# Scores of four head groups in one go in a shifted-attention stage, and its bias product moved to the second group

## The chip, the cores and the metric

The kernel runs on one core of one Trainium2 chip. The metric is the device time of one launch in microseconds (us). Three runs of the kernel before gave 1269.83, 1270.92 and 1271.11 us; their median is 1270.92 us.

## The reference, cut to what matters

The whole program is an audio tower: a convolutional tokenizer with its own attention, a shifted-window attention, a slice attention, a bidirectional GRU and a mixture of experts, each added to the running activations `h` of shape (64, 128, 64). The change touches the shifted-window attention alone. Its input is the layernorm of `h` (64 sequences of 128 rows by 64 channels); with a sequence as long as the window there is no shift and no mask:

```python
qkv = x @ qkv_weight.T + qkv_bias            # 64 sequences, 8 heads of 8 channels
attn = einsum("whqd,whkd->whqk", q * 8 ** -0.5, k) + bias_table[rel_idx]   # 128 x 128 for each head
attn = softmax(attn, axis=-1)
out = einsum("whqk,whkd->wqhd", attn, v) @ proj_weight.T + proj_bias
```

All is in float32.

## The kernel before

The program is written by hand, one instruction list for each engine, with semaphores between them. In the attention stage (stage 2) the 64 sequences are taken two at a time: 32 pairs of sequences, and since a loop turn `i` holds two of them (lanes `l` = 0 and 1), 16 turns. The two sequences of a pair have 16 heads in all, 4 in each of four head groups `u` = 0 to 3. A group's scores are 128 queries by 4 x 128 keys, one PSUM bank. A turn has eight slots `t` = 4 l + u, one for each group. `pipelined` writes turn 0 out, loops over turns 1 to 14, and writes turn 15 and a draining turn out.

What each engine does for group t, and in which slot:

- GpSimd, slot u = 2, for the next pair: `spread` (L614) multiplies the keys `a_k` with a mask, so that `a_kz` holds in each quarter of 32 partitions the keys of four heads, 512 columns. It waits for the keys and for all scores of the pair before (`a_sc_r`).
- TensorE: `scores` (L690) multiplies one quarter of 32 rows of `a_q` with the same quarter of `a_kz`: 32 x 128 by 32 x 512, into the bank `scores_bank(t)`. Before the change groups t+1 and t+2 are multiplied in each odd slot; groups 0 and 1 of a pair come in the last slot of the pair before, groups 2 and 3 in slot u = 1.
- The position bias is added by VectorE for groups 0, 1 and 2: `tensor_tensor_reduce` (L852), four instructions of 128 x 128, adds it, stores the sum in `a_P` and takes the extreme of each row. For group 3 TensorE adds it: `bias` (L696) multiplies the identity with the 512 columns of the bias table into the same bank, in slot u = 2, and VectorE takes the extremes in one instruction (`tensor_reduce`, L848) from the bank.
- ScalarE, one slot later: four exponentials with row sums (L799), from `a_P`, or for group 3 from the bank.
- VectorE, two slots later: reciprocal of the sums (L837); GpSimd: `normed` (L620) multiplies the probabilities.
- TensorE, three slots later: four transposes (L739) into bank 4; VectorE (even groups, L861) or ScalarE (odd groups, L804) copies them out.
- TensorE, four slots later: `attended` (L709), probabilities by values; after group 3 VectorE copies them (L868).
- For the next pair: `rows` (L668, transpose of the rows, slot 0; copied by ScalarE at L776), `qkv` (L674 to L676, slot 1), queries by ScalarE (L780) and keys by VectorE (L830, slot 1), values by ScalarE (L786, slot 3). For the pair before last: `project` (L721, slot 0), added to `h` by VectorE (L874).
- Once in a turn VectorE centres rows for the next layernorm (L275, L277, slot 5, behind the keys) and takes their variance (slot 7), ScalarE squares them (L284, slot 6), and GpSimd makes the inverse roots (L293, L295).

Each engine works through its slots strictly in the order written. In a slot TensorE has: transposes of the group three back, values (`attended`) of the group four back, qkv (slot 1), scores (odd slots), bias (slot 2); in slot 0 rows and the projection come behind the transposes, ahead of `attended`.

In stage 1a the convolutions (L159 and L171) use the array in the same way as the scores: products of 32 rows by 512 columns in four row quarters, into four banks.

Of the kernel before, what the change touches and what calls it, by code (L numbers as in the profile page):

```python
# [59 lines left out]
def build(nc, xp, consts, out):  # L60
# [8 lines left out]
    def c(name, a=0, b=None):  # L69

        o, w = ON[name]
        return cst[:, o + a:o + (w if b is None else b)]

    eye = c("eye")
# [501 lines left out]
    def exists(i, d, last=N2 - 1):  # L576

        return not isinstance(i, int) or 0 <= i + d <= last
# [16 lines left out]
    def scores_bank(t):  # L595
        return bank(SBANK[t % 4])
# [65 lines left out]
    def stage2_pe(pe, start=None):  # L662
        def rows(i, l):
            pe.wait_ge(a_xs_r, i * 2 + (l + 1))

            if l or exists(i, -1):
                pe.wait_ge(a_v_r, i * 2 + l)
            nc.tensor.transpose(bank(2)[:, 0:128], xs[l], eye).then_inc(a_t_r, 1)  # L668

        def qkv(i, l):  # L670
            pe.wait_ge(a_xT_r, i * 2 + (l + 1))

            pe.wait_ge(a_h_r, i * 2 + (l + 1))
            nc.tensor.matmul(bank(2)[:, 128:256], c("a_q"), xT[l], start=True, stop=True)  # L674
            nc.tensor.matmul(bank(3)[:, 0:128], c("a_k"), xT[l], start=True, stop=True)
            nc.tensor.matmul(bank(2)[:, 256:384], xT[l], c("a_v"), start=True, stop=True).then_inc(a_qkv_r, 1)  # L676

        def scores(i, t):
            l, u = t // 4, t % 4
            if u == 0:  # L680
                pe.wait_ge(a_q_r, i * 2 + (l + 1))
                pe.wait_ge(a_kz_r, i * 2 + (l + 1))
            if t >= 4 or exists(i, -1):

                if u == 3:
                    pe.wait_ge(a_e_r, i * 8 + (t - 3))
                else:
                    pe.wait_ge(a_mx_r, i * 8 + (t - 3))
            r = slice(32 * u, 32 * u + 32)
            m = nc.tensor.matmul(scores_bank(t), a_q[l][r, :], a_kz[l][r, :], start=True, stop=u != 3)  # L690
            if u != 3:
                m.then_inc(a_sc_r, 1)

        def bias(t):

            nc.tensor.matmul(scores_bank(t), eye, c("a_bias", 512, 1024), start=False, stop=True).then_inc(a_sc_r, 1)  # L696

        def attended(i, t):
            l, u = t // 4, t % 4
            if u % 2:  # L700
                pe.wait_ge(a_pta_r, i * 4 + (t // 2 + 1))
            else:
                pe.wait_ge(a_ptd_r, i * 4 + (t // 2 + 1))
            if u == 0:
                pe.wait_ge(a_v_r, i * 2 + (l + 1))

                pe.wait_ge(a_oT_r, i * 2 + (l + 2))
            for j in range(4):
                m = nc.tensor.matmul(bank(6)[32 * j:32 * j + 32, 128 * u:128 * u + 128], a_v[l][:, 128 * u + 32 * j:128 * u + 32 * j + 32],  # L709
                                     a_PT[t % 4][:, 128 * j:128 * j + 128], start=True, stop=True)  # L710
            m.then_inc(a_av_r, 1)

        def project(i, l):

            pe.wait_ge(a_oT_r, i * 2 + (l + 1))

            pe.wait_ge(a_h_r, i * 2 + (l + 1))
            for s in range(2):
                for g in range(2):
                    for half in (0, 64):  # L720
                        m = nc.tensor.matmul(bank(3)[half:half + 64, 128 + 64 * s:192 + 64 * s],  # L721
                                             a_oT[l][:, 128 * (2 * s + g) + half:128 * (2 * s + g) + half + 64], a_pp[:, 64 * g:64 * g + 64],
                                             start=(g == 0), stop=(g == 1))
            m.then_inc(a_pr_r, 1)

        def slot(i, t):
            l, u = t // 4, t % 4
            if i_is(i, 0) and t == 1:

                pe.wait_ge(b_h, ND)  # L730
            ib, tb = back(i, t, 3)
            if exists(ib, 0):
                pe.wait_ge(a_n_r, ib * 8 + (tb + 1))
                if tb % 2:
                    pe.wait_ge(a_ptd_r, ib * 4 + (tb // 2 + 1))
                elif tb or exists(ib, -1):
                    pe.wait_ge(a_pta_r, ib * 4 + tb // 2)
                for k in range(4):
                    m = nc.tensor.transpose(bank(4)[:, 128 * k:128 * (k + 1)], a_P[tb % 4][:, 128 * k:128 * (k + 1)], eye)  # L739
                m.then_inc(a_pt_r, 1)  # L740
            ib, tb = back(i, t, 4)
            if u and exists(ib, 0):
                attended(ib, tb)
            if u == 1 and exists(i, l, N2 - 1):
                qkv(i + l, 1 - l)
            if t % 2:
                for d in (1, 2):
                    if exists(i, (t + d) // 8):
                        scores(i + (t + d) // 8, (t + d) % 8)
            if u == 2 and exists(i, 0):  # L750
                bias(t + 1)
            if u == 0:
                if exists(i, l, N2 - 1):
                    rows(i + l, 1 - l)
                if exists(i, -1, N2 - 1):
                    project(i, l)
                if exists(ib, 0):
                    attended(ib, tb)
            if isinstance(i, int) and i == N2 and t < 2:
                stage3_pe(pe, start=t)  # L760
        if start == 0:
            rows(0, 0)
            return
        if start == 1:
            qkv(0, 0)
            return
        pe.wait_ge(f_dve, SETUP3)
        pe.wait_ge(m_loaded, LOADED7)
        scores(0, 0)
        scores(0, 1)  # L770
        pipelined(pe, slot)

    def stage2_act(act, start=None):
# [15 lines left out]
        def slot(i, t):  # L789
            l, u = t // 4, t % 4  # L790
            ib, tb = back(i, t, 1)
            if exists(ib, 0):
                act.wait_ge(a_mx_r, ib * 8 + (tb + 1))
                if tb % 4 == 3 and (tb >= 4 or exists(ib, -1)):
                    act.wait_ge(a_pt_r, ib * 8 + (tb - 3))
                for k in range(4):
                    P = a_P[tb % 4][:, 128 * k:128 * (k + 1)]
                    raw = scores_bank(tb)[:, 128 * k:128 * (k + 1)] if tb % 4 == 3 else P
                    m = nc.scalar.activation(P, raw, ACT.Exp, bias=a_mx[tb % 4][:, k:k + 1], scale=-1.0, accum_out=a_sm[tb % 4][:, k:k + 1])  # L799
                m.then_inc(a_e_r, 1)  # L800
            ib, tb = back(i, t, 3)
            if tb % 2 and exists(ib, 0):
                act.wait_ge(a_pt_r, ib * 8 + (tb + 1))
                nc.scalar.copy(a_PT[tb % 4], bank(4)).then_inc(a_pta_r, 1)  # L804
            if u == 0 and exists(i, l, N2 - 1):
                rows(i + l, 1 - l)
            if u == 1 and exists(i, l, N2 - 1):
                queries(i + l, 1 - l)
            if u == 3 and exists(i, l, N2 - 1):
                values(i + l, 1 - l)  # L810
            if i_is(i, 0) and t in (2, 4):
                g = LATE[t // 2 - 1]
                square(act, g + 1, 8 * g, 8, g % 2)
            if t == 6 and exists(i, -1):
                square(act, i + LN[1], i * 4 - 4, 4, 0)
            if isinstance(i, int) and i == N2 and t in (0, 2):
                stage3_act(act, start=t // 2)
# [9 lines left out]
    def stage2_dve(v, start=None):  # L827
# [4 lines left out]
        def slot(i, t):  # L832
            l, u = t // 4, t % 4
# [6 lines left out]
                v.wait_ge(b_c3, ND)  # L840
            if exists(i, 0):

                v.wait_ge(a_sc_r, i * 8 + (t + 1))
                if u != 3 and (t >= 4 or exists(i, -1)):
                    v.wait_ge(a_pt_r, i * 8 + (t - 3))

                if u == 3:
                    m = nc.vector.tensor_reduce(a_mx[t % 4], scores_bank(t).rearrange("p (j k) -> p j k", j=4), X, ALU.min)  # L848
                else:
                    nc.vector.memset(spare[:, 24 + t:25 + t], 0.0)  # L850
                for k in range(0 if u == 3 else 4):
                    m = nc.vector.tensor_tensor_reduce(a_P[t % 4][:, 128 * k:128 * (k + 1)], scores_bank(t)[:, 128 * k:128 * (k + 1)],  # L852
                                                       c("a_bias", 512 * (u % 2) + 128 * k, 512 * (u % 2) + 128 * (k + 1)), 1.0, 3e38,
                                                       ALU.add, ALU.min, a_mx[t % 4][:, k:k + 1])
                m.then_inc(a_mx_r, 1)
# [1476 lines left out]
```

## Time and profile before

| | us |
|---|---|
| median of the three runs | 1270.92 |
| the profiled execution, its own time | 1270.48 |
| its span on the core | 1268.2 |
| TensorE busy (matmuls) | 1169.8, 92% of the span |
| VectorE busy | 846.8, 67% |
| ScalarE busy | 757.4, 60% |
| GpSimd busy | 618.4, 49% |

The span is the time from the first to the last instruction that the profile holds; the rest of the execution's time lies around it. An engine's busy time sums what its records cover; records of TensorE overlap, so that a busy TensorE is not one at its peak. The granted clock is the share of TensorE's full clock that it was given in a stretch: 1.00 is 2.4 GHz, 0.50 is 1.2 GHz. In lists, PE is TensorE, DVE VectorE, ACT ScalarE, POOL GpSimd, and L690 is line 690 of the kernel. The value behind an arrow in square brackets is the idle time of the engine just before the group, and what ended it.

### The profile page before, as it was taken

To read this page: it belongs to the slowest core of one execution; us is meant where nothing else is said; L and a number is where in the kernel's file an instruction comes from. 1 tells how busy PE (TensorE), PEld (TensorE's weight loads), DVE (VectorE), ACT (ScalarE), POOL (GpSimd) and SP (SyncE) were. 2 spreads that over 40 slices of the span, in tenths; PEclk is the share of its full clock that TensorE was granted. 3 is DMA by queue.
4 is the path that set the end of the run, shared out by engine and by line. 5 is a ranking of instruction groups with operands and counts; after the bars stand their busy time and mean duration, and the time that the engine had idled before them with its cause. 6 is when DMAs were issued, how large, how long until landed. Compare 5 with 4: busy or idle time off the path is not lost.

```text
span 1268.2 us, 43497 instructions
## 1 busy us (share of the span) xinstructions
PE 1169.8 (92%) x16184; PEld 806.1 (64%) x16184; DVE 846.8 (67%) x2765; ACT 757.4 (60%) x2435; POOL 618.4 (49%) x939
## 2 busy tenths in 40 slices
PE   7989989999999979999999998899999999789997
PEld 3447745555555547787878877677777764456665
DVE  5965667777777767787787876555555555746664
ACT  0137678888888855555555554566666666544553
POOL 6012567676667753555565565233333332245455
PEclk9988989999999989999999999999999999889999
DMA  6000000000000000000000000000000000000000
GB/s 229 1 1 2 2 2 1 0 0 0 0 0 0 0 2 3 2 0 0 0 0 0 0 0 2 2 1 0 0 0 0 0 1 1 1 5 16 17 17 18
DMA packets 10833, 10.26 MB, mean 8 GB/s; under 512 B 9232, under 2 KB 9872, under 8 KB 10640
## 3 DMA queue, kind: packets, MB, share of 16 engines
q1 hardware_dynamic: 10768, 9.35, 2.5%
q8 instruction: 46, 0.75, 0.3%
q14 instruction: 19, 0.16, 0.0%
HBM read 7.25 MB, written 2.10 MB: 7 GB/s over the span
## 4 chain that ended last, share of the span: by engine, by line
PE 65%; issue 12%; POOL 11%; DVE 6%; ACT 4%; POOLq 1%; DMA 0%; SPq 0%; ACTq 0%; DVEq 0%
PE bank L1489 8%; POOL big L620 7%; PE bank L1837 5%; PE bank L1171 5%; PE bank L1855 5%; PE bank L1484 5%; PE bank L1160 3%; PE bank L1472 3%; PE bank L159 3%; PE bank L1249 3%; PE bank L1180 3%; PE bank L1198 2%; PE bank L1602 2%; PE bank L1239 2%; PE bank L1219 2%
## 5 line engine op out<-in xcount | busy, mean ns | idle before, releaser
L620 POOL TENSOR_TENSOR big<-big 128x512 f32<-128x512 f32 x128 | 132.9, 1039 | 55.7 <-DVE big L837 55.7
L799 ACT ACTIVATE big<-big 128x128 f32<-128x128 f32 x384 | 148.9, 394 | 0.5 <-DVE big L852 0.5
L1074 POOL TENSOR_TENSOR big<-big 128x512 f32<-128x512 f32 x64 | 65.6, 1045 | 127.3 <-DVE big L1348 127.3
L1570 POOL TENSOR_TENSOR big<-g_a,g_b 64x64 f32 x128 | 40.1, 313 | 172.4 <-DVE g_a L1560 172.4
L1551 DVE TENSOR_TENSOR_SCAN g_t<-g_zero_r,bank 128x128 f32<-128x128 f32 x128 | 53.8, 420 | 87.6 <-ACT g_zero_r L1536 87.6
L739 PEld LDWEIGHTS bank<-cst,big 128*128 128x128 f32 x512 | 57.2, 142 | 76.6 <-issue 59.9
L1758 POOL TENSOR_TENSOR big<-big 128x512 f32<-128x512 f32 x48 | 61.0, 1270 | 72.9 <-DVE big L1961 70.3
L1891 ACT ACTIVATE big<-bank 128x512 f32<-128x512 f32 x128 | 66.1, 604 | 48.7 <-PE bank L1837 48.7
L1536 ACT ACTIVATE g_zero_r<-bank,g_bias 128x64 f32<-128x64 f32 x128 | 40.7, 318 | 90.0 <-PE bank L1489 89.9
L852 DVE CUSTOM_DVE_ANT_0 big<-bank,cst 128x128 f32<-128x128 f32 x384 | 88.4, 286 | 6.9 <-issue 6.9
L690 PE MATMUL bank<-big 32*128 32x512 f32 x256 | 76.1, 646 | 15.2 <-POOL big L614 8.0
L739 PE MATMUL bank<-cst,big 128*128 128x128 f32 x512 | 83.7, 286 | 3.6 <-POOL big L620 2.9
L1489 PEld LDWEIGHTS bank<-g_b,cst 128*64 128x64 f32 x1024 | 40.3, 136 | 57.9 <-DVE g_b L1558 57.6
L1171 PEld LDWEIGHTS bank<-big 128*128 128x128 f32 x512 | 61.2, 196 | 24.3 <-issue 23.5
L1855 PEld LDWEIGHTS bank<-cst,big 128*64 128x64 f32 x2048 | 62.4, 138 | 18.5 <-issue 17.4
L799 ACT ACTIVATION_READ_ACCUMULATOR big<-big 128x1 f32 x384 | 74.0, 193 | 0.0
L1489 PE MATMUL bank<-g_b,cst 128*64 128x64 f32 x1024 | 57.9, 234 | 10.9 <-DVE g_b L1558 10.6
L1855 PE MATMUL bank<-cst,big 128*64 128x64 f32 x2048 | 66.6, 223 | 0.0
L1294 ACT ACTIVATE big<-big 128x1024 f32<-128x1024 f32 x32 | 33.9, 1059 | 54.7 <-DVE big L1339 54.7
L1171 PE MATMUL bank<-big 128*128 128x96 f32 x512 | 66.5, 284 | 0.0
L1837 PE MATMUL bank<-big,cst 64*128 64x512 f32 x256 | 65.9, 631 | 0.0
L1961 DVE TENSOR_TENSOR big<-bank,fB 128x512 f32<-128x512 f32 x64 | 44.3, 692 | 30.1 <-PE bank L1855 28.5
(274 smaller groups left out, 3216.5 us busy)
## 6 DMA issues: line engine op xcount, KB each, us to landing
cst<-consts_dram SPq DMA_DIRECT2D x1, 3364.5 KB, 14.2
out_dram<-h SPq DMA_DIRECT2D x8, 256.0 KB, 2.6
big<-x_dram SPq DMA_DIRECT2D x3, 512.0 KB, 5.8
cst<-consts_dram SPq DMA_DIRECT2D x3, 256.0 KB
big<-x_dram SPq DMA_DIRECT2D x1, 513.0 KB, 4.2
big<-consts_dram SPq DMA_DIRECT2D x4, 96.0 KB, 2.2
cst<-consts_dram SPq DMA_DIRECT2D x4, 48.0 KB, 2.0
g_ih_exchanged<-consts_dram SPq DMA_DIRECT2D x2, 96.0 KB, 7.3
```

What stands on the lines that cost most here:

```text
L620: nc.gpsimd.tensor_tensor(P, P, a_rs[t % 4].unsqueeze(2).to_broadcast([128, 4, 128]), ALU.mult).then_inc(a_n_r, 1)
L690: m = nc.tensor.matmul(scores_bank(t), a_q[l][r, :], a_kz[l][r, :], start=True, stop=u != 3)
L739: m = nc.tensor.transpose(bank(4)[:, 128 * k:128 * (k + 1)], a_P[tb % 4][:, 128 * k:128 * (k + 1)], eye)
L799: m = nc.scalar.activation(P, raw, ACT.Exp, bias=a_mx[tb % 4][:, k:k + 1], scale=-1.0, accum_out=a_sm[tb % 4][:, k:k + 1])
L852: m = nc.vector.tensor_tensor_reduce(a_P[t % 4][:, 128 * k:128 * (k + 1)], scores_bank(t)[:, 128 * k:128 * (k + 1)], c("a_bias", 512 * (u ...
L1074: nc.gpsimd.tensor_tensor(w, w, f_rs[l][:, 8 * s:8 * s + 8].unsqueeze(2).to_broadcast([128, 8, 64]), ALU.mult).then_inc(f_w_r, 1)
L1171: m = nc.tensor.matmul(regions()[:, k // 4, k % 4, :], f_w[l][:, 128 * k:128 * k + 128], f_xs1[l][:, 96 * (k // 4):96 * (k // 4) + 96], st ...
L1484: nc.tensor.matmul(to[:, ::-1, 1, :] if s else to[:, :, 0, :], w, x, start=((half == 0 or gate == 2) and s == 0), stop=True, skip_group_ch ...
L1489: m = nc.tensor.matmul(to[64 * d:64 * d + 64, :], c("g_hh", 128 * gate + 64 * d, 128 * gate + 64 * d + 64), state[:, :], start=start, stop ...
L1837: nc.tensor.matmul(hidden_bank(s, e), c("m_w1", 128 * e, 128 * e + 128)[64 * s:64 * s + 64], m_xT[l][64 * s:64 * s + 64, :], start=True, s ...
L1855: m = nc.tensor.matmul(out_bank(e)[64 * half:64 * half + 64, 64 * (2 * p + s):64 * (2 * p + s) + 64], hidden(e, s)[:, 128 * p + 64 * half: ...
L1891: nc.scalar.activation(hidden(e, s), hidden_bank(s, e), ACT.Relu).then_inc(m_ra, 1)
```

## The change

The scores of a pair's four groups are multiplied one behind the other in slot 0 of the pair itself, ahead of everything else of TensorE in that slot, each in its own row quarter and into its own bank. The one bias product goes from group 3 to group 1 and stands right behind them. VectorE's single reduction and ScalarE's exponentials from the bank go to group 1 with it; group 3 is now treated as groups 0 and 2 are. The waits of the scores are changed: they wait for the maxima of all four groups of the pair before and the exponentials of its group 1. VectorE's group 0 waits for the first of the four products, the other groups for all of them and the bias. The wait for the end of stage 1b (`b_h`) moves from slot 1 to slot 0.

```diff
-        def scores(i, t):
-            l, u = t // 4, t % 4
-            if u == 0:
-                pe.wait_ge(a_q_r, i * 2 + (l + 1))
-                pe.wait_ge(a_kz_r, i * 2 + (l + 1))
-            if t >= 4 or exists(i, -1):
-
-                if u == 3:
-                    pe.wait_ge(a_e_r, i * 8 + (t - 3))
-                else:
-                    pe.wait_ge(a_mx_r, i * 8 + (t - 3))
-            r = slice(32 * u, 32 * u + 32)
-            m = nc.tensor.matmul(scores_bank(t), a_q[l][r, :], a_kz[l][r, :], start=True, stop=u != 3)
-            if u != 3:
-                m.then_inc(a_sc_r, 1)
-
-        def bias(t):
-
-            nc.tensor.matmul(scores_bank(t), eye, c("a_bias", 512, 1024), start=False, stop=True).then_inc(a_sc_r, 1)
+        def scores(i, l):
+
+            pe.wait_ge(a_q_r, i * 2 + (l + 1))
+            pe.wait_ge(a_kz_r, i * 2 + (l + 1))
+            if l or exists(i, -1):
+                pe.wait_ge(a_mx_r, i * 8 + 4 * l)
+                pe.wait_ge(a_e_r, i * 8 + (4 * l - 2))
+            for u in range(4):
+                r = slice(32 * u, 32 * u + 32)
+                m = nc.tensor.matmul(scores_bank(u), a_q[l][r, :], a_kz[l][r, :], start=True, stop=u != 1)
+                if u != 1:
+                    m.then_inc(a_sc_r, 1)
+
+            nc.tensor.matmul(scores_bank(1), eye, c("a_bias", 512, 1024), start=False, stop=True).then_inc(a_sc_r, 1)
...
-            if i_is(i, 0) and t == 1:
+            if i_is(i, 0) and t == 0:
 
                 pe.wait_ge(b_h, ND)
+            if u == 0 and exists(i, 0):
+                scores(i, l)
...
-            if t % 2:
-                for d in (1, 2):
-                    if exists(i, (t + d) // 8):
-                        scores(i + (t + d) // 8, (t + d) % 8)
-            if u == 2 and exists(i, 0):
-                bias(t + 1)
...
-        scores(0, 0)
-        scores(0, 1)
         pipelined(pe, slot)
...
-                if tb % 4 == 3 and (tb >= 4 or exists(ib, -1)):
+                if tb % 4 == 1 and (tb >= 4 or exists(ib, -1)):
                     act.wait_ge(a_pt_r, ib * 8 + (tb - 3))
                 for k in range(4):
                     P = a_P[tb % 4][:, 128 * k:128 * (k + 1)]
-                    raw = scores_bank(tb)[:, 128 * k:128 * (k + 1)] if tb % 4 == 3 else P
+                    raw = scores_bank(tb)[:, 128 * k:128 * (k + 1)] if tb % 4 == 1 else P
...
-                v.wait_ge(a_sc_r, i * 8 + (t + 1))
-                if u != 3 and (t >= 4 or exists(i, -1)):
+                v.wait_ge(a_sc_r, i * 8 + (4 * l + (4 if u else 1)))
+                if u != 1 and (t >= 4 or exists(i, -1)):
                     v.wait_ge(a_pt_r, i * 8 + (t - 3))
 
-                if u == 3:
+                if u == 1:
                     m = nc.vector.tensor_reduce(a_mx[t % 4], scores_bank(t).rearrange("p (j k) -> p j k", j=4), X, ALU.min)
                 else:
                     nc.vector.memset(spare[:, 24 + t:25 + t], 0.0)
-                for k in range(0 if u == 3 else 4):
+                for k in range(0 if u == 1 else 4):
```

## Rows read from the trace of the kernel before

**Rows 1.** Busy time by stretch; columns: PE, PEld, DVE, ACT, POOL, granted clock, DMA

```profile
160.00:200.00 40.00, 34.90 (x248) 18.09 (x244) 26.65 (x149) 30.20 (x140) 24.70 (x28) 0.87 0.01 2
200.00:440.00 240.00, 226.52 (x2114) 126.51 (x2114) 177.82 (x1009) 209.97 (x986) 170.02 (x213) 1.00 0.00 0
```

**Rows 2.** Waits, 200 to 440 us: total us, times, longest

```profile
POOL big L620 <- DVE big L837: 42.7, 39, 1.9
...
POOL big L614 <- PE bank L696: 25.8, 27, 1.3
...
ACT big L780 <- PE bank L676: 17.8, 26, 0.7
```

**Rows 3.** Timeline of TensorE's matmuls, one pair; columns: start us, length us

```profile
301.07 1.23 PE L690 MATMUL bank<-big 32*128 32x512 f32 x4 [0.43 <-issue]
302.23 0.66 PE L739 MATMUL bank<-cst,big 128*128 128x128 f32 x4
...
304.97 0.49 PE L674 MATMUL bank<-big,cst 128*128 128x128 f32 x2
...
305.83 1.13 PE L690 MATMUL bank<-big 32*128 32x512 f32 x4
306.89 0.66 PE L739 MATMUL bank<-cst,big 128*128 128x128 f32 x4
...
307.84 1.12 PE L696 MATMUL bank<-cst 128*128 128x512 f32 x2
308.81 0.60 PE L739 MATMUL bank<-cst,big 128*128 128x128 f32 x4
...
310.33 0.81 PE L690 MATMUL bank<-big 32*128 32x512 f32 x2 [0.57 <-POOL big L614]
```

**Rows 4.** Timeline of the other engines in the same pair

```profile
305.94 0.37 ACT L780 ACTIVATE big<-bank,a_bqs 128x128 f32<-128x128 f32 x1 [0.72 <-PE bank L676]
...
306.20 0.39 ACT L799 ACTIVATE big<-big 128x128 f32<-128x128 f32 x1
...
307.08 0.17 DVE L837 RECIPROCAL big<-big 128x4 f32<-128x4 f32 x1
...
307.34 1.04 POOL L620 TENSOR_TENSOR big<-big 128x512 f32<-128x512 f32 x1 [1.93 <-DVE big L837]
...
307.74 0.56 ACT L804 COPY big<-bank 128x512 f32<-128x512 f32 x1
...
309.05 1.04 POOL L614 TENSOR_TENSOR big<-big,a_mask 128x512 f32<-128x512 f32 x1 [0.67 <-PE bank L696]
```

**Rows 5.** Groups by shape, 200 to 440 us: count, busy us, mean ns

```profile
L739 PE MATMUL bank<-cst,big 128*128 128x128 f32 x420 | 67.7, 283 | 0.0
...
L799 ACT ACTIVATE big<-bank,big 128x128 f32<-128x128 f32 x108 | 38.2, 369 | 0.3
```

**Rows 6.** Timeline of TensorE in stage 1a, four products in four row quarters

```profile
60.12 1.14 PE L159 MATMUL bank<-big,cst 32*128 32x512 f32 x8 [0.96 <-DVE big L207]
```

**Rows 7.** Busy time by stretch in the stage's filling, clock in the third column from the end

```profile
170.00:173.20 3.20, 3.20 (x20) 2.27 (x20) 1.73 (x12) 1.82 (x10) 2.84 (x3) 0.50 0.00 0
...
183.60:190.30 6.70, 6.70 (x25) 3.12 (x24) 1.84 (x13) 4.03 (x18) 1.27 (x2) 0.50 0.01 2
```

**Rows 8.** Timeline of TensorE in the stage's filling

```profile
165.55 0.66 PE L739 MATMUL bank<-cst,big 128*128 128x128 f32 x4 [1.08 <-POOL big L620]
...
182.10 0.66 PE L739 MATMUL bank<-cst,big 128*128 128x128 f32 x4 [1.51 <-POOL big L620]
...
184.20 2.08 PE L690 MATMUL bank<-big 32*128 32x512 f32 x4
186.21 1.12 PE L739 MATMUL bank<-cst,big 128*128 128x128 f32 x4
...
187.84 2.08 PE L696 MATMUL bank<-cst 128*128 128x512 f32 x2
189.71 0.92 PE L739 MATMUL bank<-cst,big 128*128 128x128 f32 x4
```

## The prediction

> **What bounds the kernel now.** I read the stage's stretches first. Shifted attention runs from about 160 to 455 us; in its even part, 200 to 440 us, TensorE shows 94% busy, ScalarE 87%, VectorE 74%, GpSimd 71%, and the granted clock is 1.00 [rows 1]. No engine is full by that alone, so the second view is the list of waits: GpSimd's spreading of the keys (L614) waits for the bias product once a pair, and ScalarE's queries (L780) wait for the qkv products once a pair, 0.68 us each time [rows 2]. The third is TensorE's timeline over one pair [rows 3]. Read from start to start, it pauses only ahead of the scores of groups 0 and 1, 0.43 us at 301.07 and 0.57 us at 310.33, where the releaser is L614. That is a closed loop, and its terms are: scores of groups 0 and 1, 1.16 (301.07 to 302.23); the block of transposes, rows, projection, values, transposes, values, 2.74 (to 304.97); qkv 0.86; scores of groups 2 and 3, 1.06; transposes and values 0.95; bias product 1.12 and 0.09 until L614 starts at 309.05; L614 1.04; 0.24 until 310.33 [rows 3, 4]. Sum 9.26 us. Other pairs are a little shorter: 420 transposes, 16 a pair, in 240 us are 26.25 pairs of 9.14 us [rows 5]. So now the stage is one chain: everything on TensorE in order, then the spreading, then TensorE again.
>
> **The change, part by part.** (1) Two pairs of score products become four at once. How long do four take? In stage 1a four products of 32 rows by 512 columns in four row quarters take 1.14 us [rows 6], against 1.13 for two in two quarters at 305.83 [rows 3]: two more quarters are free. The other end is that they are not, 2 x 1.06. I take 1.06 until the next work, by the row of the same shape. So TensorE gets back 1.1 us a pair. (2) The bias product goes to group 1 and stands right behind the scores, in slot 0; it costs what it did, 0.97 until the next group (307.84 to 308.81). (3) The reduction with one instruction and the exponentials that read the bank move from group 3 to group 1; the counts on VectorE and ScalarE are the same, worth nothing, for the same instructions only change places. (4) The spreading no longer waits for a late bias product; it waits for keys, which come from qkv in slot 1, and it stands on GpSimd behind the normalising (L620) of group 0. (5) The scores wait for queries, spread keys, the maxima of all four old groups and the exponentials of old group 1; behind them on TensorE stand slot 0's transposes, rows, projection and values, and so ScalarE's copies and its next exponentials. No transfer or queue of SyncE is touched.
>
> **The new chain.** The loop that ended in the bias product is open, but two others close. Both begin alike: four scores 1.06, bias 0.97, the block 2.74, qkv 0.97 until queries and keys start (304.97 to 305.94), together 5.74 us [rows 3, 4]. Their two ends:
> - By VectorE and GpSimd: keys and, in every second pair, the centring of the layernorm (L275, L277) stand ahead of group 0's reciprocal, 305.94 to 307.08, 1.14; reciprocal to L620 0.26; L620 1.04; spreading 1.04; 0.24 until the scores, as at 310.33. With the 5.74 that is 9.46. In the pair without centring this end is shorter by nearly that 1.14, and the other end decides.
> - By ScalarE: queries 0.26 (305.94 to 306.20); group 1's exponentials from the bank, 4 x 0.354 = 1.41 [rows 5]; the copy of the old group 3's transposes 0.56 and 0.09, as between bias and L614, until TensorE takes the next transposes; transposes and values 0.95, ahead of the scores in TensorE's order. 5.74 + 3.27 = 9.01.
>
> The longer of the two sets each pair: 9.46 and 9.01, mean 9.24, against 9.14 now. The term gained on TensorE is thus given back: the bias product and the scores now stand ahead of the block that everything waits for, where two of the four scores and the bias stood beside other engines' work or behind qkv. 31 pairs x 0.10 = +3 us; against the 9.26 of the pair I walked through it would be -1, and were the mean 9.33 it would be +6. Nothing more at the stage's ends, an estimate.
>
> **TensorE's clock.** In a pair of 9.24 us TensorE now has 1.06 + 0.97 + 2.74 + 0.86 + 2 x 0.95 = 7.53 us of work, so 1.7 us of idleness, all in one place: between qkv with one set of transposes and values, and the next set. Now it is the 0.43 and 0.57 us above. Do rows say what such a pause does? In the filling of this stage TensorE paused 1.08 us before 165.55 and 1.51 us before 182.10 [rows 8], between the same sort of small groups. The granted clock was then 0.50 (1.2 in place of 2.4 GHz) over 170.0 to 173.2 and over 183.6 to 190.3 [rows 7]. In the even part, without such pauses, it stayed at 1.00 for 240 us [rows 1]. What half clock costs stands in the same rows: scores, transposes with values, and bias took 184.20 to 189.71, 5.51 us, against 1.06 + 0.95 + 0.97 = 2.98: lost 0.46 us in each us. The two falls cost 1.5 and 3.1 us by that, mean 2.3. All of it is on the loop, since its 5.74 us are TensorE's. Bounds: no fall, 0; a fall in every second pair at 3.1, 48 us. Rows have two pauses over 1 us and two falls, but filling had less work around them, so I take a fall at one pair in four, 8 x 2.3 = 18 us.
>
> The Trainium skill has a rule that speaks against this change more strongly ("TensorE: Matmul & The Clock Gate", Part 4: PE-mode transpose): transposes on TensorE do not count as work that keeps its clock up. By it the stretch between qkv and the next scores, where half of what runs is transposes, would nearly always bring a fall, and the sum would be the third rival's. The pauses at 165.55 and 182.10 both stood beside transposes, and both were followed by a fall, so the trace does not contradict it.
>
> **Sum.** The profiled execution took 1270.48 us (span 1268.2), 0.4 under the median of 1270.92. 1270.5 + 3 + 18 = 1291.5 us, and I say 1291.
>
> **Rivals.**
> - The clock stays at 1.00. The pauses are 1.7 us in each 9.2, and TensorE's share of work is 82%, more than in the filling. Then 1270.5 + 3 = 1273.5, or with its own bounds 1269 to 1277. Chance 0.22.
> - Faster: the pairs shorten to what ScalarE needs. Place: the keys, queries and exponentials of the next pair; if slots slide so that L620 of group 0 and the centring no longer stand ahead of the spreading when it is wanted, nothing closes before ScalarE's own 87% of 9.14, 8.0 us. Price 31 x 1.14 = 35 us, 1235; half way 1253. It decides once both loops are under 9.1 (they would be 9.46 and 9.01 as I read them). For it: TensorE has 1.1 us less to do, and ScalarE idles 0.68 us a pair on L780 alone. Against: these loops are made of the program's own orders, and I find nothing in them that overlaps. Chance 0.15.
> - The clock falls around nearly every pause: 31 x 1.5 = 46 us and 3, 1320. Chance 0.08.
> - The change does not do what it says, the four quarters run as two and two: 31 x 1.06 = 33 us and 3, 1306, and fewer pauses. The row of 1.14 us speaks against it. Chance 0.03.
> - My forecast, some falls, 1278 to 1312: chance 0.52.
>
> **Range and chances.** 0.2%, 2.5 us, is about what a measurement of this kernel can tell from no change. Slower by more: forecast 0.52, the last two 0.11, and of the first rival over half, 0.12: 0.75. Within: 0.10 (the rest of the first). Faster by more: 0.15. The range leaves out the faster rival's larger part below and the top of the falls above: 1268 to 1314.
>
> **What would show it.** Right: the four products of a pair in one group of some 1.15 us; period over two pairs 18.3 to 18.6 us outside the falls; TensorE idle 1.4 to 1.8 us once a pair, released by L620 or the spreading or ScalarE's copy; the granted clock under 1.00 over 200 to 440 us; ScalarE's busy share no higher than 87%. Wrong: a clock of 1.00 all through (then the term of 18 us is void), a period under 9 us (then a loop is not closed as I say), or the idleness spread over several short waits.

## The result, and the profile after

The changed kernel takes 1299.29 us in the median of four runs (1297.11 to 1300.98), against 1271.01 us before: slower, ratio 1.0205, with an interval of 1.0151 to 1.0258. (The ratio goes by the means; a fourth run of the kernel before took 1280.62 us and pulls it down, by the medians it is 1.022.) The forecast was 1291 us with a range of 1268 to 1314, and slower at 0.75. The profiled execution took 1297.64 us, its span is 1295.5 us, 27.3 us over the span before.

The stage's even part after, busy time by stretch with the columns of [rows 1], and below it one stretch in which the clock was never taken down, and two in which it was:

```profile
160.00:200.00 40.00, 30.50 (x257) 16.60 (x258) 28.37 (x154) 31.63 (x150) 27.34 (x32) 0.88 0.01 2
200.00:440.00 240.00, 199.75 (x1924) 112.28 (x1923) 157.31 (x898) 184.51 (x875) 149.22 (x187) 0.88 0.00 0
...
326.90:350.60 23.70, 18.59 (x216) 11.38 (x212) 17.86 (x103) 20.14 (x98) 17.63 (x22) 1.00 0.00 0
350.80:354.10 3.30, 3.30 (x11) 0.76 (x4) 1.67 (x12) 1.84 (x11) 1.99 (x4) 0.50 0.00 0
361.00:367.70 6.70, 6.44 (x43) 3.16 (x39) 2.50 (x13) 3.67 (x18) 2.83 (x5) 0.50 0.00 0
```

The granted clock over 200 to 440 us is 0.88 where it was 1.00, and since it has two levels, 24% of these 240 us, about 57 us, were at half clock. Every engine is less busy per microsecond than in [rows 1], TensorE at 83%. The other engines have not become slower, they wait more: GpSimd's spreading takes 1.04 us before and after.

TensorE's timeline in the full-clock stretch, to be held against [rows 3]:

```profile
331.29 0.66 PE L736 MATMUL bank<-cst,big 128*128 128x128 f32 x4 [1.53 <-ACT big L793]
...
332.24 1.14 PE L687 MATMUL bank<-big 32*128 32x512 f32 x8
...
334.27 0.60 PE L736 MATMUL bank<-cst,big 128*128 128x128 f32 x4
...
336.83 0.49 PE L674 MATMUL bank<-big,cst 128*128 128x128 f32 x2
...
340.29 0.66 PE L736 MATMUL bank<-cst,big 128*128 128x128 f32 x4 [1.73 <-POOL big L620]
...
341.62 1.14 PE L687 MATMUL bank<-big 32*128 32x512 f32 x8 [0.31 <-issue]
342.69 1.13 PE L691 MATMUL bank<-cst 128*128 128x512 f32 x2
343.65 0.60 PE L736 MATMUL bank<-cst,big 128*128 128x128 f32 x4
...
346.21 0.49 PE L674 MATMUL bank<-big,cst 128*128 128x128 f32 x2
...
349.48 0.66 PE L736 MATMUL bank<-cst,big 128*128 128x128 f32 x4 [1.54 <-ACT big L793]
...
350.42 1.00 PE L687 MATMUL bank<-big 32*128 32x512 f32 x4
```

L687 is the four scores, L691 the bias product, L736 the transposes, L674 the first qkv product. Four scores take 1.14 us, as the four convolutions in [rows 6]. One pause a pair, 1.73 us released by GpSimd's normalising (L620) and 1.53 us released by ScalarE's copy (L793), in turn. The pairs last 9.38 us (332.24 to 341.62) and 8.80 us (to 350.42). Their mean, 9.09, is just under the 9.14 of before. Even at full clock the change gains next to nothing.

What a pair costs when the clock is down, the same view a little earlier:

```profile
319.21 0.66 PE L736 MATMUL bank<-cst,big 128*128 128x128 f32 x4 [1.73 <-POOL big L620]
...
320.54 2.09 PE L687 MATMUL bank<-big 32*128 32x512 f32 x8 [0.21 <-issue]
322.56 2.08 PE L691 MATMUL bank<-cst 128*128 128x512 f32 x2
```

From start to start the scores hold TensorE for 2.02 us in place of 1.07. GpSimd's spreading (L614), which starts once a pair, shows the length of that pair (its own rows, in order):

```profile
308.07 1.04 POOL L614 TENSOR_TENSOR big<-big,a_mask 128x512 f32<-128x512 f32 x1
...
319.11 1.04 POOL L614 TENSOR_TENSOR big<-big,a_mask 128x512 f32<-128x512 f32 x1
...
330.75 1.04 POOL L614 TENSOR_TENSOR big<-big,a_mask 128x512 f32<-128x512 f32 x1
...
340.19 1.04 POOL L614 TENSOR_TENSOR big<-big,a_mask 128x512 f32<-128x512 f32 x1
...
348.99 1.04 POOL L614 TENSOR_TENSOR big<-big,a_mask 128x512 f32<-128x512 f32 x1
```

11.04 and 11.64 us with the clock down in them, 9.44 and 8.80 without. Over the whole stage 17 of the 31 distances are lengthened in this way.

### The profile page after: what moved, and what is told of

It reads as the page before. It is cut to its first block, busy times and chain, and to the rows that moved or that the text cites. A ratio compares the mean times of both kernels' runs of the same rounds, so it can differ in the third digit from the quotient of the medians.

```text
span 1295.5 us, 43486 instructions
## 1 busy us (share of the span) xinstructions
PE 1159.6 (90%) x16184; PEld 801.8 (62%) x16184; DVE 846.1 (65%) x2765; ACT 754.2 (58%) x2435; POOL 616.9 (48%) x939
## 4 chain that ended last, share of the span: by engine, by line
PE 62%; issue 14%; POOL 11%; DVE 6%; ACT 4%; POOLq 1%; DMA 0%; SPq 0%; ACTq 0%; DVEq 0%
PE bank L1478 8%; POOL big L620 7%; PE bank L1826 5%; PE bank L1160 5%; PE bank L1844 5%; PE bank L1473 4%; PE bank L1149 3%; PE bank L1461 3%; PE bank L1238 3%; PE bank L159 3%; PE bank L1169 3%; PE bank L1187 2%; PE bank L1591 2%; PE bank L1228 2%; PE bank L1208 2%
## 5 line engine op out<-in xcount | busy, mean ns | idle before, releaser
L620 POOL TENSOR_TENSOR big<-big 128x512 f32<-128x512 f32 x128 | 133.0, 1039 | 118.1 <-DVE big L826 118.0
L736 PE MATMUL bank<-cst,big 128*128 128x128 f32 x512 | 85.4, 291 | 54.3 <-POOL big L620 28.3
L736 PEld LDWEIGHTS bank<-cst,big 128*128 128x128 f32 x512 | 62.8, 149 | 97.3 <-POOL big L620 38.6
L788 ACT ACTIVATION_READ_ACCUMULATOR big<-big 128x1 f32 x384 | 79.9, 208 | 0.0
L793 ACT COPY big<-bank 128x512 f32<-128x512 f32 x64 | 38.0, 594 | 53.7 <-PE bank L736 53.7
L1478 PE MATMUL bank<-g_b,cst 128*64 128x64 f32 x1024 | 57.9, 234 | 10.9 <-DVE g_b L1547 10.6
```

The source lines that it names most:

```text
L620: nc.gpsimd.tensor_tensor(P, P, a_rs[t % 4].unsqueeze(2).to_broadcast([128, 4, 128]), ALU.mult).then_inc(a_n_r, 1)
L1478: m = nc.tensor.matmul(to[64 * d:64 * d + 64, :], c("g_hh", 128 * gate + 64 * d, 128 * gate + 64 * d + 64), state[:, :], start=start, stop ...
```

## The experiments

Theory: the chain of a pair is about as long as before, and the loss is TensorE's half clock, brought on by the pause. Main rivals: the chain itself is longer; or TensorE's sum of work is what counts. The kernels below ran on three chips, each time with the kernel before beside them on the same chip (medians of 1269.2 to 1270.6 us); a ratio is against that one. Clocks and pair lengths are of each kernel's profiled execution, the granted clock over 200 to 440 us where nothing else is said. Pair lengths are the distances between starts of L614. All kernels compute the whole result, except the one without the bias product. The diffs are cut to what matters, and are against the changed kernel where nothing else is said.

### Idle work in the pause

```diff
+            if u == 2 and exists(i, l, N2 - 1):      # TensorE, behind the values of slot 2
+                pe.wait_ge(a_k_r, i * 2 + (l + 2))   # bank 3 has been read
+                for _ in range(3):
+                    nc.tensor.matmul(bank(3)[:, 256:512], eye, c("a_bias", 512, 768), start=True, stop=True)
```

> The changed kernel, with three idle products added to TensorE once a pair, in its long pause (slot 2, behind the values): identity by 256 columns of the bias table into an unused part of bank 3, 3 x 0.43 = 1.3 us of 1.5 to 1.7 us of pause, 31 pairs, 40 us of work more. Clock theory (the 27 us came from half clock that the pauses bring): the granted clock in the even part goes back to 1.00, pairs of 9.44 and 8.80 us as in the full-clock stretches of the changed kernel, mean 9.12, so 1270 us, faster than the changed kernel by 27 us although it works more. Rival (the new chain itself is longer, the clock is an effect beside it): the clock may rise, but the pairs stay at 10.1 us, 1297 us, or more by what of the 40 us does not fit into the pause.

Measured: 1266.72 us, 0.9962 of before (0.9944 to 0.998). TensorE does 1.3 us more in each pair, and the kernel is some 32 us faster than the changed one. The even part's busy times, and the spreading:

```profile
200.00:440.00 240.00, 233.12 (x2322) 144.34 (x2321) 177.56 (x1015) 209.37 (x991) 169.95 (x213) 1.00 0.00 0
```

```profile
323.29 1.04 POOL L614 TENSOR_TENSOR big<-big,a_mask 128x512 f32<-128x512 f32 x1
...
332.04 1.04 POOL L614 TENSOR_TENSOR big<-big,a_mask 128x512 f32<-128x512 f32 x1
...
341.43 1.04 POOL L614 TENSOR_TENSOR big<-big,a_mask 128x512 f32<-128x512 f32 x1
```

The clock is 1.00, and the pairs are 8.75 and 9.39 us, as in the full-clock stretch of the changed kernel. The chain is not what made it slow; the clock is.

The same in every second pair only (`if t == 2` in place of `if u == 2`):

> The changed kernel with the three idle products only in the first pair of each loop turn (slot 2), so every second pause stays. Clock theory: part of the falls goes, part stays; pairs without a half-clock stretch at 9.4 and 8.75 us as with the filler everywhere. Between 1266 and 1299 us, near the middle, 1283. Rival (any idle work anywhere helps by something else than the clock, say by the queue): the gain would be half of it, but the granted clock would not follow.

Measured: 1279.03 us, 1.0078 (1.0052 to 1.0104).

```profile
200.00:440.00 240.00, 215.32 (x2106) 127.28 (x2107) 168.50 (x969) 197.68 (x939) 161.43 (x202) 0.95 0.00 0
```

The granted clock is 0.95, and only every second pair is ever lengthened, one of those of 8.75 us. Time and clock follow the number of pauses left.

One idle product in place of three:

> The changed kernel with one idle product of 0.43 us in each pause in place of three. Work on TensorE goes up by a third of the filler, the pause falls from 1.5 to 1.7 us to 1.1 to 1.3 us. Clock theory: the kernel that has pauses of 0.8 to 0.9 us (bias product on group 2, slot 1) kept its clock in nearly all of the even part, the one with 1.5 to 1.7 us lost it in every second pair, so this one stands between: a few falls, 1270 to 1280 us. Rival (only the sum of TensorE's work or the three products together matter): no difference from the changed kernel, 1299 us.

Measured: 1267.78 us, 0.9986 (0.996 to 1.0013), granted clock 0.99. Better than expected: 0.43 us of work is nearly as good as 1.3 us. TensorE's pauses in it:

```profile
321.34 0.66 PE L736 MATMUL bank<-cst,big 128*128 128x128 f32 x4 [1.10 <-POOL big L620]
...
330.49 0.66 PE L736 MATMUL bank<-cst,big 128*128 128x128 f32 x4 [0.91 <-ACT big L797]
```

In its profiled execution a single pair of the even part was lengthened, and one in the filling.

The control, three idle products in the kernel before:

> The kernel before, with the same three idle products in the same slot. Control for the price of the filler where TensorE has no pause: the loop of before holds all of TensorE's work, so each pair should be longer by nearly 1.28 us, 10.4 us, and the kernel 1271 + 31 x 1.28 = 1311 us. If it stays near 1271, TensorE's work was not on the loop of before and the reading of the old chain is wrong.

Measured: 1310.1 us (two runs), 1.031 (1.0272 to 1.0348), with the clock at 1.00. Two of its spreadings:

```profile
329.02 1.04 POOL L614 TENSOR_TENSOR big<-big,a_mask 128x512 f32<-128x512 f32 x1 [1.96 <-PE bank L696]
...
339.50 1.04 POOL L614 TENSOR_TENSOR big<-big,a_mask 128x512 f32<-128x512 f32 x1 [2.54 <-PE bank L696]
```

A pair lasts 10.48 us (10.41 in the next), 1.3 us more than before. The same work that brought 32 us back in the changed kernel costs 39 us in this one. It shows that TensorE's work was on the loop of before, one for one.

### Do transposes count?

Against the kernel with three idle products:

```diff
-                    nc.tensor.matmul(bank(3)[:, 256:512], eye, c("a_bias", 512, 768), start=True, stop=True)   # x3
+                    nc.tensor.transpose(bank(3)[:, 256:384], c("a_bias", 512, 640), eye)                       # x12
```

> The changed kernel, with twelve idle transposes of 128 columns in the same place, 12 x 0.11 = 1.3 us as well. If transposes count for the clock as products do: as with the products, clock 1.00 and 1270 us. If they do not count (the rule of the Trainium skill's page TensorE: Matmul & The Clock Gate): the clock keeps falling, 0.88 in the even part, and the time stays at 1297 us or goes above it, since at half clock the twelve take twice as long and no longer fit.

Measured: 1265.78 us, 0.9963 (0.9949 to 0.9977), clock 1.00. After one idle product had proved enough, twelve transposes were too strong a dose to tell a full share from a third, so four were run, 0.44 us:

> The changed kernel with four idle transposes of 128 columns in each pause, 0.44 us, as much as the one idle product of 0.43 us that was enough to keep the clock (1267.8 us). The twelve transposes were three times as much as was needed, and could have kept the clock also if they counted for a third. If transposes count for the clock as products do: clock 0.99 to 1.00 in the even part and 1268 us. If they count for much less, or not at all (the skill's rule on transposes): the falls come back, 0.88 to 0.95 and 1280 to 1299 us.

Measured: 1267.08 us, 0.9983 (0.9969 to 0.9998).

```profile
200.00:440.00 240.00, 209.64 (x2237) 126.25 (x2235) 175.01 (x1003) 206.76 (x979) 167.03 (x208) 0.99 0.00 0
```

The clock is 0.99, two pairs of the even part are lengthened, and the time cannot be told from the one product's 1267.78. As filler among products, transposes kept the clock as products of the same length did; no run has a stretch of transposes alone. The third rival rested on the rule of the Trainium skill ("TensorE: Matmul & The Clock Gate", Part 4) that they do not count; these runs say otherwise for idle transposes in such a pause, and the measurement decides.

### The bias product's place

Without it (group 1 gets no position bias; idle products as in the first experiment):

```diff
-                m = nc.tensor.matmul(scores_bank(u), a_q[l][r, :], a_kz[l][r, :], start=True, stop=u != 1)
-                if u != 1:
-                    m.then_inc(a_sc_r, 1)
-
-            nc.tensor.matmul(scores_bank(1), eye, c("a_bias", 512, 1024), start=False, stop=True).then_inc(a_sc_r, 1)
+                m = nc.tensor.matmul(scores_bank(u), a_q[l][r, :], a_kz[l][r, :], start=True, stop=True)
+                m.then_inc(a_sc_r, 1)
```

> The changed kernel with the filler, and without the bias product on TensorE: group 1's scores get no position bias. By my chains the 0.97 us stand in both of them, between the scores and the block: pairs of 9.39 - 0.97 = 8.4 and 8.75 - 0.97 = 7.8, but no pair can be under what ScalarE needs, 8.0, so mean 8.2 against 9.07, 31 x -0.87 = -27 us, 1240 us. Rival (the bias product stands beside other engines' work, TensorE has idleness left): no change against the filler alone, 1267 us.

Measured: 1237.51 us, 0.976 (0.9731 to 0.9789). Its spreading:

```profile
324.35 1.04 POOL L614 TENSOR_TENSOR big<-big,a_mask 128x512 f32<-128x512 f32 x1
...
332.19 1.04 POOL L614 TENSOR_TENSOR big<-big,a_mask 128x512 f32<-128x512 f32 x1
...
340.75 1.04 POOL L614 TENSOR_TENSOR big<-big,a_mask 128x512 f32<-128x512 f32 x1
```

7.84 and 8.56 us, 0.91 and 0.83 less than with it. The product behind the scores is on both chains, for nearly its whole 0.97 us. The 8.0 us that I gave ScalarE as a floor are its busy time in the mean of two pairs, and I was wrong to hold a single pair against them: 7.84 lies under, since ScalarE squares rows only in every second pair. The mean of 8.20 lies above, so whether pairs can go under ScalarE's busy time was not tested.

On group 2, behind qkv in slot 1 (VectorE's single reduction and the exponentials from the bank go to group 2 too):

```diff
-                pe.wait_ge(a_e_r, i * 8 + (4 * l - 2))
+                pe.wait_ge(a_e_r, i * 8 + (4 * l - 1))
...
             if u == 1 and exists(i, l, N2 - 1):
                 qkv(i + l, 1 - l)
+            if u == 1 and exists(i, 0):
+                bias()                        # scores_bank(2), eye, c("a_bias", 0, 512)
...
-                v.wait_ge(a_sc_r, i * 8 + (4 * l + (4 if u else 1)))
+                v.wait_ge(a_sc_r, i * 8 + (4 * l + (1, 2, 4, 3)[u]))
```

> The changed kernel with the bias product taken off group 1: it goes to group 2, and stands in slot 1 behind qkv (VectorE's single reduction and the exponentials from the bank go to group 2 too). By the loops the bias product's 0.97 us leaves the stretch between scores and qkv; then the next wait is that the scores need group 2's exponentials, and my sum for a pair at full clock is 8.9 us, 31 x 0.25 = 8 us less than before, 1263 us with no fall of the clock. Since a pause of over 1 us stays, falls are to be expected, some half as many as now, so 1263 to 1280 us. Rival (the place of the bias product does not matter, only TensorE's sum of work): pairs as in the changed kernel, 1297 us.

Measured: 1258.45 us, 0.9901 (0.9863 to 0.9939), better than expected: pairs of 8.20 and 9.07 us, granted clock 0.99. TensorE's pauses are in other places and short:

```profile
321.12 1.14 PE L687 MATMUL bank<-big 32*128 32x512 f32 x8 [0.62 <-ACT big L791]
...
328.21 0.66 PE L737 MATMUL bank<-cst,big 128*128 128x128 f32 x4 [0.81 <-ACT big L796]
...
329.61 1.14 PE L687 MATMUL bank<-big 32*128 32x512 f32 x8 [0.38 <-ACT big L791]
```

The scores now wait for the exponentials (L791), 0.4 to 0.6 us, as was foreseen: the bank that ScalarE reads belongs to a group one later. Two idle products in slot 2 on top:

> Bias product on group 2 and in slot 1 behind qkv, with two idle products (0.86 us) in slot 2. The same kernel without them had pairs of 8.19 and 9.07 us and one fall of the clock in its even part, and the clock was down again behind it. Clock theory: the pairs stay as they are (mean 8.63), the fall goes, some 2 to 4 us less than without, 1255 us. Rival (idle products now stand in the way, since this chain has a shorter pause): pairs 0.3 us longer, 1268 us.

Measured: 1252.9 us, 0.9869 (0.9847 to 0.989), clock 1.00, pairs still 8.20 and 9.07. Of all versions that compute the result it is the fastest, 1.3% under the kernel before. The bias product in the pause itself, with no idle work:

```diff
+            if u == 2 and exists(i, 0):
+                bias()                        # slot 2, behind the transposes, group 2
```

> Bias product on group 2, placed in slot 2 behind the transposes, so that it stands in the pause itself and needs no idle work. Clock theory: granted clock 1.00 in the even part. Chains: the product leaves the stretch from scores to qkv, but group 2's reduction waits for it, which stands in VectorE's order ahead of group 1's reciprocal; my sum is 8.8 us a pair, 1270 - 31 x 0.35 = 1260 us. Rival (work in the pause delays the transposes and scores behind it as much as it spares): 9.1 us a pair, 1269 us.

Measured: 1255.5 us, 0.9875 (0.9826 to 0.9924), clock 0.99, pairs 8.19 and 9.12 us. The clock fell once in the even part, at its very end. This kernel beats the one before and the changed one without a single idle instruction, so that the clock also holds without the wait that stands ahead of the idle products; it and the one above cannot be told apart by their intervals.

Left with group 3 in slot 2, as before, only the scores merged (two runs; lines against the changed kernel):

```diff
-                pe.wait_ge(a_e_r, i * 8 + (4 * l - 2))
+                pe.wait_ge(a_e_r, i * 8 + 4 * l)
...
+            if u == 2 and exists(i, 0):
+                bias()                        # scores_bank(3), eye, c("a_bias", 512, 1024)
```

> Only the first half of the change: four scores at once in slot 0, but the bias product stays with group 3 and in slot 2, as before. Now the scores of a pair have to wait for the exponentials of the old group 3, which ScalarE makes in slot 0 of the same pair. Theory: the exponentials that read the bank must not belong to the last group; this wait closes a longer chain, some 10.6 us a pair, 1271 + 31 x 1.44 = 1316 us, and more where the longer pause brings the clock down, up to 1370 us. Rival (the merged scores alone carry the effect of the change, the move of the bias adds the loss): faster than the changed kernel, 1270 to 1290 us.

Measured: 1347.59 us, 1.0608 (1.0539 to 1.0676), clock 0.88. Its pairs without a fall take 10.3 and 10.6 us, against 10.6 expected; the rest is the clock. The scores wait for ScalarE's exponentials of the last group, and the pause is longest of all:

```profile
300.89 1.14 PE L687 MATMUL bank<-big 32*128 32x512 f32 x8 [2.41 <-ACT big L791]
```

So the move away from group 3 was needed for the merge; that it went as far as group 1, and into slot 0, was not.

### The centring's place

With the idle products, VectorE's centring in slot 4 in place of slot 5 (`if t == 4 and exists(i, -1)`):

> The changed kernel with the filler, and the layernorm's centring on VectorE moved from slot 5 (behind the keys) to slot 4. Theory of the two chains: in the pair with centring the keys, the reciprocal, the normalising and the spreading come up to 0.87 us earlier, and then another chain (ScalarE's, 8.75 in the other pair) sets that pair: 9.39 becomes 8.8 to 9.0, mean 8.85, 31 x -0.2 = -6 us against the filler alone (1267), 1260 us. Rival (the centring is not on the chain): the same time as with the filler alone.

Measured: 1269.98 us, 1.0001 (0.998 to 1.0023): expected 1260, missed. The pair with centring became shorter, by 0.34 where 0.4 to 0.6 was expected, and yet it did not pay: 9.05 in place of 9.39, but 9.25 in place of 8.75. TensorE's only long pause, once in two pairs, shows who was late instead:

```profile
302.82 0.66 PE L736 MATMUL bank<-cst,big 128*128 128x128 f32 x4 [0.73 <-DVE big L854]
```

The centring now stands ahead of VectorE's own copy of the transposes (L854), for which TensorE's next transposes wait. My sum had followed the keys and left out that copy. The rival, that centring is not on the chain, falls as well: both pairs changed. The mean went from 9.07 to 9.15 us, 31 x 0.08 = 2.5 us, most of what the time lies over the 1266.7 of the idle products alone.

## Why the prediction was right, and what was off

- **The old chain** was read rightly: with three idle products a pair became 10.4 to 10.5 us long, and 31 x 1.28 us gave 1311 against 1310.1 measured.
- **Four scores in the time of two** held: 1.14 us, 1.07 until the bias product.
- **The two new chains** are there, with their releasers (L620 and L793) in turn. Sizes: the one by VectorE and GpSimd was put at 9.46 and measured 9.38, the one by ScalarE at 9.01 and measured 8.80; together 18.18, just under the 18.3 to 18.6 named as a sign. The term that was too large is the block from transposes to values: I took 2.74 us from a pair of the kernel before. In the changed kernel it lasts 2.56 (334.27 to 336.83, and 343.65 to 346.21). Against it stood L614 to scores, 0.39 in place of 0.24. So the chain term of +3 us was negative: in the even part the mean pair at full clock is 9.07 us against 9.15 before, 31 x -0.08 = -2.5 us.
- **The clock** decided, as forecast, and the mechanism held in each link: one pause of 1.5 to 1.7 us a pair, a clock under 1.00, scores, bias and transposes nearly twice as long. Its size was put too low: 18 us forecast, some 32 measured (1299.3 less 1266.7 or 1265.8, taking the two filled kernels for the changed one without falls). The forecast came on top of a kernel that had two falls of its own in its filling, 1.5 and 3.1 us by the same price; on top of them the falls cost some 28. The step that failed is "a fall at one pair in four": 17 of the 31 pairs were lengthened. The 31 distances between starts of L614 add up to 314.7 us, against 282.1 in the kernel with three idle products. Of these 32.6 us 3.0 lie in the filling, 24.9 in the 22 pairs from 206 to 431 us and 4.7 at the end, 1.9 for each lengthened pair. The price stood: 57 us at half clock, times the 0.46 of the text, are 26 us. I had argued that the filling of before was emptier and the even part would fall more rarely; the pause counted, and the fullness around it did not save it.
- **The rivals.** A clock of 1.00 was the case only with work put into the pause. The faster rival never opened in this kernel, since the bias product sits on both chains; without that product the pairs come to 8.2 on average, and with it on group 2 the times of 1253 to 1258 us lie near the 1253 that the rival had called half way. Two and two quarters: excluded by the 1.14 us. A fall at nearly every pause with 1320 us: too much, and the rule named for it, that transposes don't count, did not hold for the filler.
- That the sum came out near (1291 for 1299) is in part luck: the chain term erred upward by some 6 us and the clock term downward by some 10. About 3 us more lie at the stage's ends, where I had put nothing; no run took them apart.

Left open: why one idle product or four transposes are enough when the pause that stays is still 1.1 us; falls are then rare, one or two in 240 us, but there. Nor does any run separate the length of a single pause from the sum of TensorE's idleness in a pair: each filler shortens both, and the kernels on group 2 have both less idleness and shorter pauses than the changed one. Why the block of transposes to values became shorter is open as well.

## What to carry to other kernels

Where TensorE's work is merged or taken away, ask where its idleness goes: before the change there were pauses of some 0.5 us and no fall in the even part; gathered into one pause of 1.5 to 1.7 us a pair it cost some 32 us, where the change brought 2.5 us at full clock. Look at the granted clock before explaining a slowdown by the chain, and test it with idle work in the pause, which cost nothing there: the pairs with it are as long as the changed kernel's at full clock. An operation that many things queue behind belongs behind them, if its own reader is late enough: the bias product cost 0.87 us a pair right behind the scores (9.07 against 8.20 without it), and some 0.45 on group 2, behind qkv or in the pause (8.64 and 8.66), where the scores wait 0.4 to 0.6 us for group 2's exponentials.

## What the runs showed of the hardware

- 0.43 us of idle products, or 0.44 us of idle transposes, in a pause of 1.5 to 1.7 us brought the granted clock of the even part from 0.88 to 0.99, and the kernel from 1299 to between 1267 and 1268 us.
- Idle transposes did that as well as idle products: 1267.08 and 1267.78 us, a clock of 0.99 with either.
- Pauses of 1.5 to 1.7 us, one in each pair, brought the clock to half for 24% of the time; not every such pause did, as the stretch from 326.9 to 350.6 us shows, with three of them at 1.00.
- From the scores to what follows, four 32 x 512 products in four row quarters took TensorE 1.07 us at full clock and 2.02 at half; two in two quarters took 1.06 (305.83 to 306.89).
- The block from transposes to values, the same six groups, took 2.74 us in the kernel before and 2.56 in the changed one behind the bias product; in the kernel with the bias product in slot 2, where the block follows the scores, it took 2.62 (303.48 to 306.10).
